# A hybrid block with three attentions: one preparing block ahead of each attention, and the first heads' rows stored first

## What is computed

```
x = x + time_mix(layernorm(x))                 # a recurrence over tokens
x = x + ffn(layernorm(x))                      # F
x = x + latent_attention(layernorm(x))         # L, causal
x = x + ffn(layernorm(x))                      # H

def ffn(x):                                    # x is already normalised once
    h = layernorm(x) * ln1_g + ln1_b           # normalised a second time
    q, k, v = h @ Wq, h @ Wk, h @ Wv           # 16 heads of 8 channels
    x = x + softmax(q @ k.T / sqrt(8)) @ v @ Wo
    m = layernorm(x) * ln2_g + ln2_b
    return x + top2_of_8_experts(m)

layernorm: (x - mean) / sqrt(var + 1e-5)
latent_attention: q, k, v from products of W_dq, W_uq, W_dkv, W_uk, W_uv, W_o
```

## Time and profile before

| | |
|---|---|
| median of 3 runs | 2895.62 us (2891.0 to 2900.37) |
| the profiled execution | 2897.65 us |
| its span, first to last instruction | 2895.7 us |
| busy: TensorE, DVE, ACT, POOL | 2541.8, 2035.4, 1662.0, 401.2 us |
| mean granted clock of TensorE | 0.901 of full |

### The profile page before, as it was taken

How to read it: one execution, slowest core, us unless ns; L and a number is a source line. 1 busy time by engine, 2 the same in 40 slices (tenths; PEclk the granted TensorE clock), 3 DMA queues, 4 the chain that set the end, 5 groups by cost and what they waited for, 6 DMA issues and landing times. The chain is left out here.

```text
span 2895.7 us, 52883 instructions
## 1 busy us (share of the span) xinstructions
PE 2541.8 (88%) x15633; PEld 1298.5 (45%) x15633; DVE 2035.4 (70%) x3105; ACT 1662.0 (57%) x3397; POOL 401.2 (14%) x646
## 2 busy tenths in 40 slices
PE   5788874999999999959489999967999999999766
PEld 2688873333333333349344444423333333333466
DVE  5544445888888888353378888846888888887253
ACT  4222211377777788815237667651687777777624
POOL 1322201000000000027201111111000000000045
PEclk8888876699999999969769999976999999999868
DMA  1000002010110010025221111103100110110135
GB/s 43 1 1 0 0 0 73 23 31 19 26 29 24 20 29 22 1 68 175 57 91 38 43 31 44 37 1 87 23 23 23 29 27 17 29 29 8 43 92 168
DMA packets 52841, 110.52 MB, mean 38 GB/s; under 512 B 10474, under 2 KB 28356, under 8 KB 46596
## 3 DMA queue, kind: packets, MB, share of 16 engines
q1 hardware_dynamic: 44500, 96.13, 13.1%
q0 software_dynamic: 4992, 10.23, 1.1%
q10 hardware_dynamic: 3248, 2.84, 0.5%
HBM read 84.39 MB, written 20.84 MB: 36 GB/s over the span
## 5 line engine op out<-in xcount | busy, mean ns | idle before, releaser
L528 DVE TENSOR_REDUCE Fmaxes<-Fm 128x1 f32<-128x1024 f32 x512 | 603.1, 1220 | 98.0 <-PE Fm L293 96.4
L528 DVE TENSOR_REDUCE Hmaxes<-Hm 128x1 f32<-128x1024 f32 x512 | 603.1, 1220 | 97.9 <-PE Hm L293 96.4
L442 ACT ACTIVATE Hprob<-Hs 128x512 f32<-128x512 f32 x1024 | 529.1, 603 | 121.6 <-PE Hs L305 121.0
L442 ACT ACTIVATE Fprob<-Fs 128x512 f32<-128x512 f32 x1024 | 529.1, 603 | 121.5 <-PE Fs L305 121.0
L305 PE MATMUL Fs<-Fqa,Fka 64*128 64x512 f32 x1024 | 410.9, 467 | 5.5 <-ACT Fprob L442 5.2
L305 PE MATMUL Hs<-Hqa,Hka 64*128 64x512 f32 x1024 | 410.8, 467 | 5.5 <-ACT Hprob L442 5.2
L951 ACT ACTIVATE Lprob<-Ls 128x512 f32<-128x512 f32 (+3 forms) x640 | 302.0, 540 | 133.4 <-PE Ls L829 132.4
L293 PE MATMUL Hm<-Hka,Hqa 64*128 64x512 f32 x1024 | 350.3, 460 | 18.1 <-DMA Hka<-Hparts 11.2
L293 PE MATMUL Fm<-Fka,Fqa 64*128 64x512 f32 x1024 | 350.2, 460 | 18.0 <-DMA Fka<-Fparts 11.3
L293 PEld LDWEIGHTS Fm<-Fka,Fqa 64*128 64x128 f32 x1024 | 161.8, 194 | 277.0 <-DVE Fmaxes L528 258.6
L293 PEld LDWEIGHTS Hm<-Hka,Hqa 64*128 64x128 f32 x1024 | 161.8, 194 | 276.9 <-DVE Hmaxes L528 258.6
(11 more groups left out here) (558 smaller groups left out, 2800.1 us busy)
## 6 DMA issues: line engine op xcount, KB each, us to landing
FEw<-in_L_ffn_W SPq DMA_DIRECT2D x39, 256.0 KB, 2.8
HEw<-in_L_ffn_W SPq DMA_DIRECT2D x39, 256.0 KB
Fqa<-F_qparts SPq DMA_DIRECT2D x60, 128.0 KB
Fka<-F_kparts SPq DMA_DIRECT2D x60, 128.0 KB
Lqa<-L_qparts SPq DMA_DIRECT2D x60, 128.0 KB
Lka<-L_kparts SPq DMA_DIRECT2D x60, 128.0 KB
Hqa<-H_qparts SPq DMA_DIRECT2D x60, 128.0 KB
Hka<-H_kparts SPq DMA_DIRECT2D x60, 128.0 KB
```

The costliest lines, as they stand in the source:

```text
L442: nc.scalar.activation(prob[:, kt % PSLOTS, q0:q1], seat(kt, n)[:, 0:q1 - q0], ACT.Exp, scale=SCALE).then_inc(expd, 1)
L528: nc.vector.reduce_max(maxes[:, qt, half:half + 1], mps[j % 2][:, 0:width], AX.X)\
```

## The change

1. `prepare` takes the place of `clear_semaphores`, the two `normalize` and, at L, of `latent_weights`; at H also of `add_tokens`. In it the statistics of `x` are made once. With variance v and e = 1e-5, DVE makes v + e and (v + e) e + v, ACT the roots of both in one instruction, DVE both reciprocals; the second scales `x` directly to the twice normalised `n2`. POOL clears the old semaphores, SP waits for the late weights. At L, TensorE and ACT make the latent weights ahead of their other work.
2. `n1` is made in the second block of `attention`, by 16 DVE instructions ahead of the maxima.
3. Head 0 is loaded from DRAM like the others. Each of queries and keys is stored in two pieces, first the 16 rows of heads 0 and 1, then the other 112. SP stores the queries, ACT the keys. The loads wait for the first pieces alone.
4. The value projections are single tiles ahead of every second of the first 32 maxima items.
5. ACT does one exponential of a single column ahead of head 0.

```diff
-        def copy_queries(sp, parts, s, at, arrived):
-                sp.dma_start(qa[rows, s, :].bitcast(F32),
-                             parts[0:DH, 0, a, :].bitcast(F32).unsqueeze(1).broadcast_to([DH, PARTS, T]))
+        def load_queries(queue, h, s, at, arrived):
+                queue.dma_start(qa[rows, s, :].bitcast(F32),
+                                qscr[a, h * DH:(h + 1) * DH, :].unsqueeze(1).broadcast_to([DH, PARTS, T]))
...
-        def store(sp, parts, w, stored):
-            for half in range(2):
-                cols = slice(half * T // 2, (half + 1) * T // 2)
+        def store(queue, parts, w, first, rest):
+            for rows, stored in ((slice(0, FIRST), first), (slice(FIRST, P), rest)):
+                queue.dma_start((qscr, kscr)[w][:, rows, :].rearrange("a p t -> p a t"), parts[rows, w, :, :].bitcast(F32))\
                     .then_inc(stored, 16)
+        FIRST = 2 * DH
...
+                    act.wait_ge(split, 2 * NB)
+                    store(act, parts, 1, k_first, k_stored)
...
+                    sp.wait_ge(split, NB)
+                    store(sp, parts, 0, q_first, q_stored)
                     sp.wait_ge(cleared, 1)
-                    sp.wait_ge(split, NB)
-                    copy_queries(sp, parts, 0, LOW, low_in[0])
-                    copy_queries(sp, parts, 0, 0, top_rows_in[0])
+                    sp.wait_ge(q_first, 16)
+                    load_queries(sp, 0, 0, LOW, low_in[0])
+                    load_queries(sp, 0, 0, 0, top_rows_in[0])
...
-                    copy_keys(sp, parts, 0, LOW, low_in[0])
-                    store(sp, parts, 0, q_stored)
-                    store(sp, parts, 1, k_stored)
-                    sp.wait_ge(q_stored, 32)
-                    sp.wait_ge(k_stored, 32)
+                    sp.wait_ge(k_first, 16)
+                    load_keys(sp, 0, 0, LOW, low_in[0])
                     load(sp, 1, 1, LOW, low_in[1])
                     load(sp, 1, 1, 0, top_rows_in[1])
+                    sp.wait_ge(q_stored, 16)
+                    sp.wait_ge(k_stored, 16)
                     tops(0, 0, NB)
...
-                    for b in range(NB):
-                        project(b)
                     for j in range(NM):
+                        if j % 2 == 0 and j // 2 < NT:
+                            project(j // 2)
                         low_item(0, 0, 0, j)
...
-                    copy_keys(act, parts, 0, 0, top_rows_in[0])
+                    act.wait_ge(k_first, 16)
+                    load_keys(act, 0, 0, 0, top_rows_in[0])
...
+                    nc.scalar.activation(warm[:, :], ident[:, 0:1], ACT.Exp).then_inc(warmed, 1)
...
+                    for t in range(NT):
+                        nc.vector.tensor_scalar(n1[:, t, :], x[:, t, :], mv[:, t, 0:1], rdev[:, 0, t:t + 1],
+                                                ALU.subtract, ALU.mult).then_inc(kept, 1)
...
+                if also is not None:
+                    for b in range(NB):
+                        nc.vector.tensor_tensor(x[:, 4 * b:4 * b + 4, :], x[:, 4 * b:4 * b + 4, :], also[:, 4 * b:4 * b + 4, :],
+                                                ALU.add).then_inc(added, 1)
...
+                nc.vector.tensor_scalar(squares[:, 0, :], mv[:, :, 1], EPS_LN, None, ALU.add).then_inc(stat, 1)
+                if twice:
+                    dve.wait_ge(stat, 2 * NT + 1)
+                    nc.vector.scalar_tensor_tensor(squares[:, 1, :], squares[:, 0, :], EPS_LN, mv[:, :, 1], ALU.mult, ALU.add)
+                dve.wait_ge(root, 1)
+                nc.vector.reciprocal(inv[:, 0:two, :], dev[:, 0:two, :]).then_inc(stat, 1)
...
+                for n, (rows, out, _, _) in enumerate(steps):
+                    act.wait_ge(made, n + 1)
+                    nc.scalar.activation(out[:, :], lps[n % 4][0:rows, 0:C], ACT.Copy).then_inc(copied, 1)
+                act.wait_ge(stat, 2 * NT + two)
+                nc.scalar.activation(dev[:, 0:two, :], squares[:, 0:two, :], ACT.Sqrt).then_inc(root, 1)
...
-            normalize(nc, name + "N1", x, n1, None, consts)
-            normalize(nc, name + "N2", n1, n2, main, consts, col["ln1_g"], col["ln1_b"])
+            prepare(nc, name + "P", x, n2, main, consts, prep[name], mv, inv, col["ln1_g"], col["ln1_b"], twice=True,
+                    also=also, arrivals=arrivals)
```

More of the change, by code:

```diff
@@ L37, in semaphore, with attention @@
     return handle
[L40 to L57, removed]
+def attention(nc, name, xT, wq, wk, wv, consts, out_y, causal, x, mv, rdev, n1):
     SCALE = float(DH) ** -0.5
@@ L350, in deliver, with project @@
                         last.then_inc(scored, 1)
[L352 to L359, removed]
+                    def project(t):
+                        b, j = t // 4, t % 4
+                        if j == 0:
+                            pe.wait_ge(expd, b + 1)
+                        last = nc.tensor.matmul(ring(b - BEFORE)[:, j * P:(j + 1) * P], xT[:, t * P:(t + 1) * P],
+                                                wv[:, :], start=True, stop=True)
+                        if j == 3:
+                            last.then_inc(scored, 1)
                     def low_item(h, i, s, j):
@@ L1221, in _ @@
                 dve.wait_ge(added, NB)
-def add_tokens(nc, name, y, x):
-    with ExitStack() as ctx:
-        added = semaphore(nc, ctx, name + "added")
-        with nc.Block() as block:
-            @block.vector
-            def _(dve):
-                nc.vector.tensor_tensor(x[:, :, :], x[:, :, :], y[:, :, :], ALU.add).then_inc(added, 1)
-                dve.wait_ge(added, 1)
 TILES = 2 * NT + E_N - 1
@@ L2265 @@
 FFN_W = ["Wq", "Wk", "Wv", "Wo", "Wg"]
[L2268 to L2285 removed]
+PREPARE_SEMAPHORES = ("added", "stat", "root", "normed", "turned", "moved", "made", "copied", "swept")
@@ L2286, in _ @@
             @block.tensor
             def _(pe):
-                for n, (rows, dst, (a, b), after) in enumerate(STEPS):
-                    if after:
-                        pe.wait_ge(moved, after)
+                for n, (rows, _, (a, b), after) in enumerate(steps):
+                    if max(after, n - 3) > 0:
+                        pe.wait_ge(copied, max(after, n - 3))
                     if b is None:
-                        last = nc.tensor.transpose(ps[0:rows, n, 0:C], a[:, :], ident)
+                        last = nc.tensor.transpose(lps[n % 4][0:rows, 0:C], a[:, :], ident)
@@ L2293, in _ @@
                     else:
-                        last = nc.tensor.matmul(ps[0:rows, n, 0:C], a[:, :], b[:, :], start=True, stop=True)
+                        last = nc.tensor.matmul(lps[n % 4][0:rows, 0:C], a[:, :], b[:, :], start=True, stop=True)
                     last.then_inc(made, 1)
-            @block.vector
-            def _(dve):
-                for n, (rows, dst, _, _) in enumerate(STEPS):
-                    dve.wait_ge(made, n + 1)
-                    nc.vector.tensor_copy(dst[:, :], ps[0:rows, n, 0:C]).then_inc(moved, 1)
-                dve.wait_ge(moved, len(STEPS))
+                for t in range(NT):
+                    pe.wait_ge(normed, t + 1)
+                    last = nc.tensor.transpose(ps[t // 4][:, (t % 4) * P:(t % 4 + 1) * P], dst[:, t, :], ident)
+                    if t % 4 == 3:
+                        last.then_inc(turned, 1)
@@ L2305, in build, with _ @@
+            @block.gpsimd
+            def _(pool):
+                for handle in old:
+                    pool.sem_clear(handle)
+            @block.sync
+            def _(sp):
+                for handle, value in arrivals:
+                    sp.wait_ge(handle, value)
 def build(nc, a, table, out):
```

165 lines of the change are left out of this document (106 added, 59 removed).

## The result

The changed kernel takes **2875.1 us** (median of 4 runs, 2870.9 to 2879.7); the kernel before, run beside it, 2897.3. The ratio is 0.9927, with a 95% interval of 0.9903 to 0.9950: 22 us faster, half of the 44 that the sum gave, and outside the range. The profiled execution took 2879.73 us (span 2878.0, 17.7 less than before).

What follows compares the result with a forecast made beforehand. TensorE was busy 88% of the span, but short serial chains set the time at the attention entries and before the first maxima. 34.5 + 7.5 - 2 + 3.8 = 43.8 us gave 2852 us, forecast 2843 to 2861, range 2831 to 2868.

Steps and rivals of the forecast that it cites:

- Entries: Entries into attentions F, L and H: one block in place of three, gaining 12.3, 9.7 and 12.5, together 34.5 us.
- the exposed table load at L: Entry L: ACT loads the square-root table behind its eight copies, leaving 1.3 us exposed.
- Projections among the maxima: Head 0's maxima: interleaved value projections lose 0.5 us at F and H, 1 at L, 2 us together; DVE the fuller engine.
- TensorE bounds the maxima: Rival at head 0's maxima: projections cost 6.7 us per attention, 18 more than taken, 2870 us; chance 0.05.
- First heads' rows: Projections to first maximum: stored rows replace copies, starting 2.5 us earlier per attention, 7.5 for three (-5 to +18).
- both stores in one line with the loads: Late end for the first rows: transfers served in turn, start 1.6 us later per attention; as rival 2864 us, chance 0.18.
- ACT's out of their way: Early end for the first rows: what ACT issues (7.5 us) spares SP's queue, start 5.9 us earlier.
- Table load: Before head 0's first exponential: the 1.28 us load comes while ACT waits, gaining 3.8 us over three attentions.
- `n1`: Second block at F and H: 4.2 us of DVE work, priced at nothing; POOL's memset may delay it up to 3.5 us.
- The clock did not rise early: Rival at head 0's maxima: interleaved projections fill TensorE and the clock rises early, 17 us for three, 2835 us; chance 0.10.
- DMA at full rate: Rival on first rows: small transfers run beside large ones, start 7.4 us earlier, 22 in all, 2837 us; chance 0.12.
- The heads did not start at the lower clock for long: Rival "Slower": the clock stays at the lower level into the heads, say 2910 us; chance 0.02.

Runs made afterwards that it cites:

- root_first: Changed kernel with value projections first, large stores behind loads, POOL's memset in the first block, L's root before ScalarE's last two copies: 2832.0 us, 0.9776 of before.
- rests_last: Changed kernel with value projections ahead of the maxima and SP storing the 112 other query and key rows behind the loads: 2837.9 us, 0.9786 of before.

## Why the prediction was off

**Entries: right.** 34.4 us against 34.5; singly 12.3, 9.8 and 12.3 against 12.3, 9.7 and 12.5. The clearing is hidden, and the exposed table load at L is 1.46 us (1.3 predicted, where the text's own numbers, 4.55 + 1.28 - 4.60, give 1.2); `root_first` removed 1.0 of it.

**Projections among the maxima: the step that failed.** The term was 2 us and measured 16.2. "DVE is the fuller engine" was right for the pair as it stood (2.36 against 2.35 by record, and the prediction itself said that the ends of matmuls are modelled) and was taken as if TensorE had room for more. TensorE's own need per pair, 2.07 us, was in the earlier trace rows: with DVE's period of 2.53 there was room for 0.46 us, and the projection needs 0.73. (2.80 - 2.53) x 16 = 4.3 would have been the estimate at F and H (3.5 and 3.4 measured). The second fault was the price: 0.42 us was that of projections in a row. The third was L, costed at 1 us without reading its own loop, where the window of before has TensorE at 22.57 and DVE at 22.22 of 23.50: 9.3 us. The rival "TensorE bounds the maxima", 18 more than the sum and given 0.05, names what happened; its 6.7 us per attention is too high for F and H and too low for L.

**First heads' rows: right in sign, too large.** 7.5 us were taken. From the start of the last split to the first maximum the gain is 1.0, 0.9 and 0.6, and the other 1.5 of the 4.0 in the table lie in the projections: at H they took 8.5 us at a granted clock of 1.00, where the profile before has 10.2 us at 0.83. At F the first maximum was to come 20.8 us after the first store, and came after 22.3. The sum took a value between two ends, which were both stores in one line with the loads, or ACT's out of their way. Two 1.84 MB stores landed late (view of DMA issues: KB each, us from issue to landing), where the text had 4.9 us each:

```profile
F_qparts<-Fparts SPq DMA_DIRECT2D x1, 1792.0 KB, 10.3
...
F_kparts<-Fparts ACTq DMA_DIRECT2D x1, 1792.0 KB, 15.3
```

The same view by queue shows why, first for 467 to 474 us, then for 474 to 481 (packets, MB, share of 16 engines; q1 has what SP issues, q10 what ACT issues):

```profile
q1 hardware_dynamic: 227, 1.73, 92.8%
```

```profile
q10 hardware_dynamic: 216, 1.63, 75.8%
q1 hardware_dynamic: 100, 0.61, 23.8%
```

ACT issued its stores from 470.17 us on, but up to 474 only SP's queue moved anything, with the engines all but full. Then came ACT's, with SP's in what was left. So ACT's stores did not stay out of the way, and the prediction's terms can be put to the test: all in one line they give 22.2 + 2.7 = 24.9 us, 2.6 above the measured 22.3, and without the two large stores 15.1, where `rests_last` measured 14.95.

By the rule of the Trainium skill cited in the prediction (DMA: Bandwidth & Descriptors, "Issuing engines are not separate DMA queues") the start was to be 1.6 us later, and it came 0.9 earlier, between that and the 2.5 of the term and nearer to the term. That the transfers of both queues share the same engines, the trace bears out. `rests_last` prices the large stores, since it takes them out of the line and gains 8 us per attention. No run moves only one of the two, so how much of it is SP's store and how much ACT's stays open.

**Table load: right**, 3.5 us against 3.8. **`n1`: right.** It met the memset, took 3 us longer, and nobody waited for it.

**The other rivals.** The clock did not rise early: 0.50 through all maxima with TensorE busy 44.61 of 45.10 us. DMA at full rate would have brought the maxima 7.4 us earlier, and 0.9 came. The heads did not start at the lower clock for long: after the change F's first exponential was followed by 5.6 us at the lower level, before by 7.3.

**The profiled execution.** 43.8 was the sum; 14.2 of it went to the maxima, 3.5 to the first rows, 5.75 to the clock in the time mix and 2 to the heads, and 0.6 to small differences. By medians the last three are not part of the effect: before to after is 22 us, and with the projections put back 33 to 37. The stages of the table give 25.7 (34.4 + 4.0 - 16.2 + 3.5) and, without the projections, 41.9; what the medians lack of that isn't explained.

## What to carry to other kernels

Work put into the gaps of a busy loop is priced by what the loop's second engine has left over per turn, from that engine's own durations, and each loop is read for itself; work that stood under a long wait for a transfer was free where it was. A transfer that many wait for goes ahead of the large ones which nobody needs yet: the large stores of two issuing engines ran one after the other, and moving both back gained 8 us per attention, until the projections that had hidden there set the time. Before a difference of medians is explained, the profiles are to show the same difference in the stage that was edited.

## What was not expected of the hardware

- A projection of 128x128 between maxima of 64x128 took 0.73 us at the lower clock, 0.50 in a group of four, 0.42 in a long row.
- The granted clock stayed at its lower level (1.2 GHz) for 45.1 us with TensorE busy for 44.61 of them, and once it fell from 2.4 GHz in the middle of busy work and stayed low until the heads ended, at a cost of some 14 us.
- The issue of the same four loads took SP 7.68 us behind a store of 1.84 MB and 3.94 without it: here the large transfers in the line also delayed the engine which issues, and with it the end of a block for all engines.
- Stores issued on two engines did not run side by side: ACT's, issued from 470.17 us on, moved nothing up to 474, while SP's ran.
